# Conditional residual kernel: ACT rounds a chunk of weights behind the copies of y, chunks are dealt a slot ahead, and DVE makes the second z_lo ahead of turning x

## The reference

```python
x = x + einsum('bct,bcd->bdt', x, W0[cond])       # mixes the 64 channels of a sample
x = x + einsum('bsi,boi->bso', x, W1[adapter])    # mixes the 1024 elements
```

## Time and profile before

| | us |
|---|---|
| median of 3 runs | 823.0 (822.79 to 824.88) |
| profiled execution, its own time | 823.68 |
| its span | 822.0 |
| granted TensorE clock, mean | 0.994 |

### The profile page before, as it was taken

How to read it: one execution, slowest core, us unless ns; L and a number is a source line. 1 busy time by engine, 2 the same in 40 slices (tenths; PEclk the granted TensorE clock), 3 DMA queues, 4 the chain that set the end, 5 groups by cost and what they waited for, 6 DMA issues and landing times.

```text
span 822.0 us, 19295 instructions
## 1 busy us (share of the span) xinstructions
PE 793.1 (96%) x3448; PEld 645.4 (79%) x3449; DVE 592.2 (72%) x697; ACT 453.2 (55%) x771; POOL 250.2 (30%) x157
## 2 busy tenths in 40 slices
PE   3999999999999999999999999999999999999995
PEld 3878877688877788888777888877888888888884
DVE  5767787778778767787787778778776667666765
ACT  2446556555645655556466564655555545554554
POOL 1234434243433212335331253343112221222120
PEclk9999999999999999999999999999999999999998
DMA  6444442444342234444423444343332333233333
GB/s 177 140 122 129 142 131 85 128 139 125 115 144 71 82 102 128 130 128 119 143 68 88 131 137 141 114 128 89 88 93 74 102 99 80 76 102 99 77 80 77
DMA packets 73953, 90.89 MB, mean 111 GB/s; under 512 B 13780, under 2 KB 64468, under 8 KB 73940
## 3 DMA queue, kind: packets, MB, share of 16 engines
q1 hardware_dynamic: 63616, 57.45, 23.4%
q10 hardware_dynamic: 10324, 33.30, 15.7%
HBM read 57.15 MB, written 33.55 MB: 110 GB/s over the span
## 4 chain that ended last, share of the span: by engine, by line
PE 47%; DVE 18%; issue 16%; ACTq 6%; DVEq 5%; ACT 4%; DMA 2%; SPq 1%; POOL 0%; POOLq 0%
PE first_ps L493 8%; PE first_ps L494 8%; DVE w_turned L799 8%; PE z_ps L493 7%; PE z_ps L494 7%; PE z_ps L496 7%; PE first_ps L496 6%; DVE y L830 5%; DVE z_parts L822 4%; PE y_ps L505 4%; ACTq L205 4%; DVEq L205 2%; DMA w_nat<-in_L_cond_weight_dram 2%; ACT y L603 2%; ACTq L581 1%
## 5 line engine op out<-in xcount | busy, mean ns | idle before, releaser
L318 POOL TENSOR_TENSOR xt_lo<-x_turned,xt_hi 128x1024 fp32r<-128x1024 f32 x61 | 146.5, 2402 | 430.9 <-ACT xt_hi L585 430.8
L493 PE MATMUL z_ps<-w_hi,xt_hi 128*128 (+1 forms) x528 | 207.2, 392 | 0.2
L493 PE MATMUL first_ps<-w_hi,xt_hi 128*128 x528 | 206.6, 391 | 0.2 <-issue 0.2
L494 PE MATMUL z_ps<-w_lo,xt_hi 128*128 (+1 forms) x528 | 206.2, 391 | 0.0
L494 PE MATMUL first_ps<-w_lo,xt_hi 128*128 x528 | 205.5, 389 | 0.0
L496 PE MATMUL z_ps<-w_hi,xt_lo 128*128 (+1 forms) x512 | 199.9, 390 | 0.0
L830 DVE TENSOR_TENSOR y<-y_ps,y 64x512 f32<-64x512 f32 x256 | 176.0, 689 | 25.6 <-ACT y L603 19.8
L496 PE MATMUL first_ps<-w_hi,xt_lo 128*128 x480 | 186.8, 389 | 0.0
L585 ACT ACTIVATE xt_hi<-x_turned 128x1024 fp32r<-128x1024 f32 x66 | 70.0, 1061 | 184.5 <-issue 115.5
L822 DVE TENSOR_TENSOR z_parts<-z_ps,z_parts 64x512 fp32r<-64x512 f32 x132 | 90.9, 689 | 96.0 <-ACT z_parts L590 93.0
L603 ACT ACTIVATE y<-y_ps 64x512 f32<-64x512 f32 x256 | 150.7, 590 | 7.6 <-PE y_ps L505 2.5
(11 more groups left out here) (117 smaller groups left out, 359.4 us busy)
## 6 DMA issues: line engine op xcount, KB each, us to landing
x_in<-in_x_dram SPq DMA_DIRECT2D x536, 64.0 KB, 2.2
out_dram<-y ACTq DMA_DIRECT2D x126, 256.0 KB, 3.4
w_nat<-in_L_cond_weight_dram SPq DMA_DIRECT2D x128, 128.0 KB
w_nat<-in_L_cond_weight_dram SPq DMA_DIRECT2D x4, 512.0 KB, 6.9
w_turned<-in_L_cond_weight_dram SPq DMA_DIRECT2D x2, 512.0 KB, 8.6
y<-in_L_cond_weight_dram SPq DMA_DIRECT2D x2, 512.0 KB, 8.4
x_turned<-in_L_cond_weights_dram SPq DMA_DIRECT2D x2, 256.0 KB, 3.8
x_in<-in_x_dram SPq DMA_DIRECT2D x2, 256.0 KB, 6.4
```

Of the source, the lines that this page charges most:

```text
L318: nc.gpsimd.tensor_tensor(xt_lo[h][:], x_turned[h][:], xt_hi[h][:].bitcast(F32), ALU.subtract).then_inc(xt_lo_made, 1)
L493: nc.tensor.matmul(to, xt_hi[h][:, t, :], whi, start=(t == 0), stop=False)
L494: mm = nc.tensor.matmul(to, xt_hi[h][:, t, :], wlo, start=False, stop=last and not pair)
```

## The change

- ACT makes w_hi of the chunk behind the copies of y(s-1) instead of ahead of z of the first half, and its look-up goes with it. The store of y is issued a slot later, behind xt_hi: y(s-2) in slot s.
- DVE makes z_lo of the second half directly behind `finish_y`, and turns x of s+2 after it.
- The table gets a field CHUNKS_NEEDED (8 times the group's number). CHUNKS of a slot becomes the larger of itself and CHUNKS_NEEDED of the next slot, so that chunks missing at a group's start are made a slot before. Slot 0 can have chunks too, so SP, ACT and DVE look for them there.
- DVE completes the table instead of POOL, behind w_lo of the first six blocks; POOL waits for it ahead of its first slot.
- At the start six chunks are loaded ahead of x of slot 0 instead of four, and PE turns x of slot 0 as the seventh block. The first half of z(0) waits for seven blocks instead of five.

```diff
-FIELDS = 8
+FIELDS = 9
-        TURN_ORDER = [0, 1, 2, 3, X0, 4, 5, 6, 7]
+        TURN_ORDER = [0, 1, 2, 3, 4, 5, X0, 6, 7]
-        FOR_FIRST_HALF = 5
+        FOR_FIRST_HALF = 7
 @block.gpsimd
-            pool.wait_ge(table_moved, 16)
-            nc.gpsimd.tensor_copy(slot_row[:, 1:LOOKED_UP + 1, CHUNKS_BEFORE], slot_row[:, 0:LOOKED_UP, CHUNKS]
-                                  ).then_inc(table_ready, 1)
...
             pool.wait_ge(first_lo_made, NH * len(TURN_ORDER))
+            pool.wait_ge(table_ready, 1)
 @block.sync
-            for c in range(4):
+            for c in range(6):
                 load_first(c)
...
-            for c in range(4, CHUNKS_PER_GROUP):
+            for c in range(6, CHUNKS_PER_GROUP):
                 load_first(c)
...
             sp.sem_inc(x_loaded[0], PER_X)
+            load_chunks(0)
             slot(0, 0)
 @block.scalar
-            def slot(j, h, before, stored):
+            def slot(j, h, before, stored, past=None):
 
                 s = 2 * j + h
-                first, last = look(act, s, CHUNKS_BEFORE, CHUNKS)
                 keep_xt_hi(s + 1, 1 - h)
-                keep_chunks_hi(first, last)
+                if past is not None:
+                    store_y(past, h)
 
                 act.wait_ge(y_summed, PER_Y * before + 2)
                 keep_z_hi(s, h, 0)
 
                 act.wait_ge(y_summed, PER_Y * before + 4)
                 place_w0(s)
                 begin_y(before, 1 - h, stored)
+                keep_chunks_hi(*look(act, s, CHUNKS_BEFORE, CHUNKS))
                 keep_z_hi(s, h, 1)
-                store_y(before, 1 - h)
...
             place_w0(0)
+            keep_chunks_hi(*look(act, 0, CHUNKS_BEFORE, CHUNKS))
             keep_z_hi(0, 0, 1)
...
             with act.Fori(0, pairs_past) as i:
-                slot(i + 1, 0, 2 * i + 1, 32 * i)
-                slot(i + 1, 1, 2 * i + 2, 32 * i + 32)
+                slot(i + 1, 0, 2 * i + 1, 32 * i, 2 * i)
+                slot(i + 1, 1, 2 * i + 2, 32 * i + 32, 2 * i + 1)
+            store_y(2 * pairs_past, 0)
             begin_y(2 * pairs_past + 1, 1, 32 * pairs_past)
 @block.vector
+            nc.vector.tensor_scalar(table[:, CHUNKS_NEEDED:CHUNKS_NEEDED + 1], got[:, 0, 3:4],
+                                    float(CHUNKS_PER_GROUP), None, ALU.mult)
...
+            def turn_chunks(s):
                 first, last = look(dve, s, CHUNKS_BEFORE, CHUNKS)
                 with dve.If(last > first):
                     with dve.Fori(first, last) as k:
                         turn_chunk(k)
+
+            def slot(j, h, before):
+
+                s = 2 * j + h
+                turn_chunks(s)
                 keep_z_lo(s, h, 0)
                 finish_y(before, 1 - h)
+                keep_z_lo(s, h, 1)
                 turn_x(j + 1, h, xt_made=s + 1)
-                keep_z_lo(s, h, 1)
 
             for i in range(TURN_OF[X0]):
                 keep_first_lo(i)
+
+            dve.wait_ge(table_moved, 16)
+            nc.vector.tensor_tensor(slot_row[:, 1:LOOKED_UP, CHUNKS], slot_row[:, 1:LOOKED_UP, CHUNKS],
+                                    slot_row[:, 2:LOOKED_UP + 1, CHUNKS_NEEDED], ALU.max).then_inc(chunks_dealt, 1)
+            dve.wait_ge(chunks_dealt, 1)
+            nc.vector.tensor_copy(slot_row[:, 1:LOOKED_UP + 1, CHUNKS_BEFORE], slot_row[:, 0:LOOKED_UP, CHUNKS]
+                                  ).then_inc(table_ready, 1)
             dve.wait_ge(table_ready, 1)
...
             turn_x(0, 1)
+            turn_chunks(0)
             keep_z_lo(0, 0, 0)
```

More of the change, by code:

```diff
@@ L12 @@
 I32 = mybir.dt.int32
-FIELDS = 8
-SAMPLE_A, SAMPLE_B, STORES, GROUP, COND_A, COND_B, CHUNKS_BEFORE, CHUNKS = range(FIELDS)
+FIELDS = 9
+SAMPLE_A, SAMPLE_B, STORES, GROUP, COND_A, COND_B, CHUNKS_BEFORE, CHUNKS, CHUNKS_NEEDED = range(FIELDS)
 def conditional_residual_kernel(nc, x, cond_ids, adapter_ids, cond_w, adapter_w, out):
@@ L156, in conditional_residual_kernel @@
         table_moved = sem("table_moved")
+        chunks_dealt = sem("chunks_dealt")
         groups_made = sem("groups_made")
@@ L839, in finish_y @@
                         add(0, n, 2 * n + 2, 2)
-            def slot(j, h, before):
-                s = 2 * j + h
+            def turn_chunks(s):
                 first, last = look(dve, s, CHUNKS_BEFORE, CHUNKS)
```

## The result

| | before | changed |
|---|---|---|
| median, us | 823.1 (822.8 to 824.9, 4 runs) | 843.5 (841.8 to 844.0, 4 runs) |
| ratio, 95% interval | | 1.0243 (1.0229 to 1.0256) |
| span of the profiled execution | 822.0 | 841.3 |
| mean granted clock | 0.994 | 0.988 |

I had forecast 807.1, in a range of 803 to 813, and had given "slower" a chance of 0.04. The kernel got 20 us slower.

The account below looks back on a forecast made before the run. TensorE was taken to lose 19.9 us waiting for z_lo where DVE and ACT loop over chunks. 823.68 - 19.9 + 4.0 (group 0) = 807.8, less 0.7 to the median: 807.1 us, range 803 to 813.

Parts of the forecast that it names:

- the old loop: DVE and ACT's round in chunk slots, 12.57 us against TensorE's 11.79; forecast to become 12.01 with a chunk.
- rival E: Chunk's look-up and loop not hidden behind the copies of y; loop 14.35, about 869 us; chance 0.04.
- z_hi of the first half to the end of the copies of y: 4.20: Loop step on ACT: 4.10 from the old timeline plus 0.1, making 4.20 us.
- From the last issue to z_hi 0.20: Loop step on ACT after the store's DMA issues: 0.20 us, between ends of 0.02 and 1.80.
- rival A: ACT's look-up or chunk loop shows by 0.4 us; loop 12.4, 812.6 us; chance 0.19.
- rival D: The wait only moves: loop 12.6 as before, time within 0.3% of the kernel before; chance 0.03.
- 10.92 without a chunk: The new loop in slots without a chunk: 10.92 us, against 12.01 with one.
- the margin: Second-half z_lo ready 3.9 us before TensorE needs it; eight chunk slots use 1.8, so groups 1 to 3 lose nothing.
- a lag of 2.8: One-sample slots ahead of groups 2 and 3: TensorE 8.15 us, loop 10.92; the slot behind takes back some 2.
- group 0: First group, its chunks arriving late: forecast to lose 4.0 us, 1.2 by slot 8 and 2.8 at slot 9, not 9.9.
- rival B: Group 0 fed late: xt_lo of slot 2 holds TensorE 1.5 to 2 us, clock falls; about 811; chance 0.15.
- stores move half a slot later: Under the other edits: y of that buffer is rewritten a slot after; no cost was put on the move.

Follow-up runs that it names:

- a_store_back: The changed kernel with the store of y(s-1) put back behind z_hi of the second half, at the slot's end: 807.2 us, 0.9801.
- a_looks_ahead: The changed kernel with the store's and W0's look-ups taken ahead of the wait for turned x, nothing else moved: 805.6 us, 0.9784.
- a_held: Control: the changed kernel with one register operation added behind the look-ups of the chunks and of the group: 842.0 us, 1.0227.
- a_chunk_early: The changed kernel with ACT rounding the chunk ahead of z_hi again, behind the store: 946.9 us, 1.1518.
- a_x_first: The changed kernel with DVE turning x ahead of the second z_lo again, the store left behind xt_hi: 806.2 us, 0.9795.
- a_reload: The changed kernel with the second sample's index loaded again, and used, between the store's two DMA issues: 865.4 us, 1.0512.

## Why the prediction was wrong

**What held.** What bounded the kernel before, and that the old loop would go: w_hi follows the copies of y directly (116.30 to 116.32), its look-up hidden, as forecast; rival E did not come. TensorE's products hardly wait for z_lo any more. The Trainium skill's queue of 8 instructions ("Advanced Engine Details and Errata", Engine Queue Depths) agrees with that row, which again shows no depth.

**What failed, 1: "z_hi of the first half to the end of the copies of y: 4.20".** It measured 4.62 (111.68 to 116.30). I had read the 4.10 from rows 6, and took for granted that W0's look-up would be as short in the new order. There it comes close behind the two DMA issues, and it is longer. The chain shows it, pieces of the changed kernel (start, us, what):

```profile
109.13 0.70 ACTq L206
...
111.90 0.99 ACTq L206
```

One load, 0.99 us of the chain, between z_hi (111.68) and W0 (113.15). Over the whole kernel W0's load takes 1.07 us or more, 1.15 in the middle; in the kernel before it took 0.49, and 0.49 in a_store_back, where the stretch is 4.22, what I had forecast. A load of 0.49 is over before the two instructions of z_hi are, though there too z_hi had just been waited for; one of 1.15 is not. "From the last issue to z_hi 0.20" measured 0.35. Together with 0.06 at the store and 0.08 less elsewhere, the loop is 12.56 and not 12.01. That was rival A's mechanism (12.4) and rival D's loop, but A priced it as 812.6 us and D as no change. Both were too low, because of the next two points.

**2: "10.92 without a chunk".** I took the loop with a chunk and subtracted the chunk. But without it ACT's second z_hi is ready at 4.2 us and DVE's y ends at 5.1, a number that stood in my own text, in the next sentence. By way of y the loop was 11.2 by my prices, still under 11.79. Measured: 11.82 to 11.94; of the difference some 0.55 us is point 1's look-up and 0.1 the way from xt_hi to z_hi. It took both, the path by y and the longer look-up, to bring the quiet loop to TensorE's pace, and that turned the sign. The path alone does no harm: a_looks_ahead has it too, with the look-ups out of the way, and loses 1.9 us.

**3: the margin.** I let eight chunk slots use it up and the quiet ones refill it. A loop of 11.8 to 11.9 refills nothing; only the slot behind one of one sample does, where the loop takes 10.6 us. The old kernel had more of it in each group: its excess begins five slots into the chunks, the new one's three. Eight chunk slots at 0.77 are 6.2 us, and each of groups 1 to 3 loses some 5.0, so 1.2 us were in hand and not 3.9. And at a slot of one sample, where TensorE needs 8.15 us, the loop keeps its length: TensorE falls 3.8 to 3.9 us behind its own pace at each of slots 23, 35 and 48, 11.6 us together. I had counted a lag of 2.8 at two of the three, with "takes back some 2" (it is 1.2). The wait that shows is not the one I watched: y of slot 22 waits for DVE to finish y of slot 21, at 313.42. Behind it the granted clock falls, as rows 10 had shown once; windows of the changed kernel (columns as in rows 10):

```profile
317.00:319.00 2.00, 2.00 (x6) 1.56 (x5) 0.00 (x0) 0.81 (x1) 1.11 (x1) 0.52 0.29 74
```

Near the 1.2 GHz level. It costs nothing more there, because the loop, not TensorE, sets the pace: from xt_hi to xt_hi across it (316.76 to 328.57) it is 11.81 us.

**4: group 0 and the ends.** Group 0 loses 10.0, not 4.0 (7.6 in a_held, where y of slot 0 came 1.8 us later). The stall at y of slot 1 went, as forecast: 3.95 us of excess before, none now. In its place TensorE waits for xt_lo of slot 2, rival B's place, 1.6 us in all, though its clock stays at full speed:

```profile
51.25 0.50 PE L493 MATMUL z_ps<-w_hi,xt_hi 128*128 x1 [1.32 <-POOL xt_lo L316]
```

The other 8.3 us are the loop's, from slot 2 on. The end took 3.3 us more, not nothing: the copies of the last y wait for a PE that waits 4.19 us for y of slot 64 (832.48). The start is within its scatter: y of slot 0 came at 43.4 to 47.0 us in the ten kernels with the new start, and at 43.3 to 45.6 in the four with the old one.

The edit that I costed worst is the store's: "stores move half a slot later" stood under the other edits, though its 2.25 us were a fifth of the loop that I had summed. Put back, or its look-up put ahead, the sum of the prediction holds: 805.6 to 807.2 measured, 807.1 forecast. That is agreement of different kernels with the number, and does not make the forecast right.

## What to carry to other kernels

When engines hand work round in a loop, write down each path round it, with and without the optional work, and compare the longest with the bound engine's pace; a few tenths beyond it cost every iteration, and margins are refilled only by iterations that are truly shorter. A look-up or DMA issue is free only where its sequencer has time to spare, because it runs ahead of its engine or would wait anyway; so place it in front of a wait, not between the wait's release and the next instruction of the loop. A price read from a row holds for that place in the order: W0's look-up cost 0.49 us in one and 1.15 in another. Two edits that are harmless or good alone (1.0038 and 0.9933) can close a loop together: test each undone singly.

## What was not expected of the hardware

- The time of a register load on ACT's sequencer goes with its place (loads between 60 and 780 us of each trace). In the changed kernel: 0.28 us (the number of stores, soon behind W0's load), 0.49 (chunks), 0.70 (the store's) and, for W0's, which starts 0.57 us behind the end of the second DMA issue, 1.15 (middle; 1.07 to 1.64).
- It is the place behind the issues, not the field: in the kernel before, the chunks' load stands there (0.35 us behind) and takes 1.22, W0's 0.49; in a_chunk_early the chunks' again 1.38, W0's 0.49. In a_store_back and a_x_first, where the next load starts 2 us or more behind the issues in most slots, it takes 0.49. In each of the long cases it ends about 1.6 to 1.7 us behind the last issue. Between the two issues (a_reload) a load takes 0.29. Why stays open.
- One register operation more on the look-ups made the kernel before 0.5% slower (1.0053), while on the changed one it made no difference (1.0227 against 1.0243).
